# Macaron block on one core: score products in shared PSUM rows, and a reordered start

## The reference, cut to what matters

```python
x = x + 0.5 * ffn(layernorm(x))    # 8 experts, D = F = 256
x = x + attn(layernorm(x))         # 16 heads of 16, causal
x = x + 0.5 * ffn(layernorm(x))

# ffn, for every token and all 8 experts:
weights = golden_weights(sigmoid(x @ Wr / temperature))
h = silu(x @ Wg[e]) * (x @ Wu[e])
out = sum over e of weights[e] * (h @ Wd[e])

# attn:
scores = q @ k.T / sqrt(16), causal mask to -inf
attn   = softmax(scores) ; ctx = attn @ v ; out = ctx @ Wo.T + bo
```

## Time and profile before

| | |
|---|---|
| median of 3 runs | 751.4 us (751.22 to 753.1) |
| the profiled execution | 749.88 us, span 748.1 us |
| TensorE busy | 738.6 us, 99% of the span, 4712 products |
| VectorE busy | 477.6 us, 64% |
| GpSimd busy | 416.0 us, 56% |
| ScalarE busy | 348.8 us, 47% |
| DMA | 90.20 MB, mean 121 GB/s |

### The profile page before, as it was taken

How to read it: one execution, slowest core, us unless ns; L and a number is a source line. 1 busy time by engine, 2 the same in 40 slices (tenths; PEclk the granted TensorE clock), 3 DMA queues, 4 the chain that set the end, 5 groups by cost and what they waited for, 6 DMA issues and landing times.

```text
span 748.1 us, 13854 instructions
## 1 busy us (share of the span) xinstructions
PE 738.6 (99%) x4712; PEld 586.8 (78%) x4712; DVE 477.6 (64%) x1306; ACT 348.8 (47%) x663; POOL 416.0 (56%) x497
## 2 busy tenths in 40 slices
PE   7999999999999999999999999999999999999998
PEld 6888888777787777778777778777777788888887
DVE  6978855865667748578447756965658533584333
ACT  5446346243465543756435456444364552333322
POOL 2687484454663545844555753453564655556663
PEclk9999999999999999999999999999999999999999
DMA  9455224634233544234542423635332333223321
GB/s 276 157 183 177 90 94 127 180 111 142 71 105 121 160 128 117 73 106 133 159 143 72 136 69 107 187 98 168 92 91 86 96 105 110 85 71 128 109 103 56
DMA packets 69718, 90.20 MB, mean 121 GB/s; under 512 B 13200, under 2 KB 49424, under 8 KB 69648
## 3 DMA queue, kind: packets, MB, share of 16 engines
q1 hardware_dynamic: 67456, 89.01, 38.8%
q10 hardware_dynamic: 2192, 0.32, 0.3%
HBM read 72.10 MB, written 17.04 MB: 119 GB/s over the span
## 4 chain that ended last, share of the span: by engine, by line
PE 84%; DVE 4%; DMA 2%; SPq 2%; POOL 1%; issue 1%; ACT 0%; DVEq 0%; POOLq 0%; ACTq 0%
PE ra L795 14%; PE ra L797 13%; PE ra L796 13%; PE dn L817 8%; PE dn L818 7%; PE dn L819 7%; PE ra L923 5%; PE ra L896 5%; PE ra L911 4%; PE ra L760 2%; SPq L1469 1%; PE ra L874 1%; PE ra L887 1%; PE ra L876 1%; PE ra L875 1%; PE ra L888 1%
## 5 line engine op out<-in xcount | busy, mean ns | idle before, releaser
L1386 POOL TENSOR_TENSOR hid<-hid,wb 128x512 f32<-128x512 f32 x124 | 161.3, 1302 | 161.5 <-DVE hid L1242 152.8
L1390 POOL TENSOR_TENSOR ht_lo<-hid,ht_hi 128x512 fp32r<-128x512 f32 x124 | 162.3, 1311 | 110.9 <-ACT ht_hi L1025 110.7
L795 PE MATMUL ra<-xt_hi,wgu_hi 128*128 128x512 f32 x508 | 223.0, 439 | 0.4 <-DVE mx L1293 0.4
L797 PE MATMUL ra<-xt_lo,wgu_hi 128*128 128x512 f32 x508 | 200.7, 395 | 0.0
L796 PE MATMUL ra<-xt_hi,wgu_lo 128*128 128x512 f32 x508 | 200.6, 395 | 0.0
L1293 DVE CUSTOM_DVE_ANT_0 junk<-ra,mask 128x128 bf16<-128x128 f32 (+3 forms) x256 | 120.4, 486 | 73.9 <-PE ra L896 72.9
L817 PE MATMUL dn<-wd,ht_hi 128*128 128x256 f32 x512 | 161.6, 316 | 0.5 <-POOL ht_lo L1390 0.5
L1234 DVE SCALAR_TENSOR_TENSOR hid<-hid,ra 128x512 f32<-128x512 f32 x125 | 85.7, 686 | 115.7 <-ACT hid L1017 114.7
L818 PE MATMUL dn<-wd,ht_hi 128*128 128x256 f32 x512 | 143.7, 281 | 0.0
L819 PE MATMUL dn<-wd,ht_lo 128*128 128x256 f32 x512 | 143.5, 280 | 0.0
L1025 ACT ACTIVATE ht_hi<-hid 128x512 fp32r<-128x512 f32 x124 | 78.0, 629 | 123.9 <-POOL hid L1386 104.0
(11 more groups left out here) (161 smaller groups left out, 815.6 us busy)
## 6 DMA issues: line engine op xcount, KB each, us to landing
wd<-wd_parts SPq DMA_DIRECT2D x56, 512.0 KB, 3.8
wb<-wts_rows SPq DMA_DIRECT2D x62, 256.0 KB, 3.9
qk_parts<-parts SPq DMA_DIRECT2D x32, 192.0 KB, 2.3
q_st<-qk_parts SPq DMA_DIRECT2D x96, 64.0 KB, 2.5
k_st<-qk_parts SPq DMA_DIRECT2D x96, 64.0 KB, 2.3
wd_parts<-wd SPq DMA_DIRECT2D x8, 512.0 KB, 3.1
ctx_rows<-cx SPq DMA_DIRECT2D x16, 256.0 KB, 3.0
stage<-in_Wg SPq DMA_DIRECT2D x8, 256.0 KB, 4.4
```

The lines of the kernel that those rows point to most:

```text
L795: mm(b_, w_hi, xt_hi[q % 2][:, c, :], start=c == 0, stop=False)
L797: last = mm(b_, w_hi, xt_lo[q % 2][:, c, :], start=False, stop=c == KT - 1)
L1386: nc.gpsimd.tensor_tensor(tb, tb, wb[m % NWB][:, :], ALU.mult).then_inc(hw_done, 1)
L1390: nc.gpsimd.tensor_tensor(ht_lo[n % NHT][:, :], hidden(n)[:, :], f32(ht_hi[n % NHT][:, :]), ALU.subtract).then_inc(lo_done, 1)
```

## The change

- **Maxima in shared rows.** `MAX_ROWS` lays the 16 max products of a group in ten banks as the exponentials are: for two heads, five banks: 128 then 384 of one head (two such), 256 of one and 256 of the other, and 512 alone (two such). TensorE signals once a bank; VectorE reduces each part with an instruction of its own and frees the bank after the last.
- **Exp rows.** In `LAYOUT` the 128 columns now come ahead of the 384 in the bank's order of products; columns stay where they are.
- **First rows' second half.** `x_rest` is sent from ScalarE's queue, as its first DMA, and no longer from SP's.
- **Root step.** For the first batch, three root steps become one of the old kind and one of third order (one more unlinked and four linked instructions).
- **Three tiles on VectorE.** `("ln", 0, 0)` takes tiles 0, 1 and 2; ScalarE takes tile 3. The second pair's transposes wait for both.
- **First expert by halves.** High and low parts of gate and up are made for the first hidden half (`sg`), then for the second (`sgx`, behind the second pair's eviction on ScalarE and behind its low part on VectorE). Expert 1's high part follows the first down weights on ScalarE.
- **Planner.** PERIOD is 4.5 for 4.55, the assumed lengths of the changed items follow.

```diff
-LAYOUT = [[(0, 0, 0)], [(1, 0, 0)], [(0, 1, 0), (0, 3, 384)], [(1, 1, 0), (1, 3, 384)],
+LAYOUT = [[(0, 0, 0)], [(1, 0, 0)], [(0, 3, 384), (0, 1, 0)], [(1, 3, 384), (1, 1, 0)],
           [(0, 2, 0), (1, 2, 256)]]
+MAX_ROWS = [[(0, 0, 384), (0, 2, 0)], [(1, 0, 384), (1, 2, 0)], [(0, 1, 0), (1, 1, 256)], [(0, 3, 0)], [(1, 3, 0)]]
-M0, PERIOD = 27.6, 4.55
+M0, PERIOD = 27.6, 4.5
...
-            for k in range(GH * QT):
-                put(meet[g] - PERIOD + 0.15 + 0.27 * k if b + g else meet[0] - 2.1 + 0.115 * k, ("max", b, g, k))
+            for r in range(GB):
+                put(meet[g] - PERIOD + 0.15 + 0.43 * r if b + g else meet[0] - 2.1 + 0.184 * r, ("max", b, g, r))
...
+        if e == 0:
+            add("act", ("sg", 0), 0.55, ("sp", "ld", 0))
+            add("act", ("sgx",), 0.55, ("sp", "ld", 0), then=[("act", "xt", 0, 1)])
+            add("dve", ("sg", 0), 0.62, ("act", "sg", 0), port=True, then=[("dve", "ln", 0, 0)])
+            add("dve", ("sgx",), 0.62, ("act", "sgx"), port=True, then=[("dve", "xt", 0, 1)])
+        else:
+            add("act", ("sg", e), 1.0, ("sp", "ld", e), then=[("act", "sd", 0)] if e == 1 else [])
...
-            row = (0.232, 0.232, 0.285, 0.285, 0.236)
+            row = (0.232, 0.232, 0.235, 0.235, 0.236)
...
                     if kind == "max":
-                        mm(o[:, 0:(i + 1) * P], q_st[0:KROWS, G % NST, hh, i * P:(i + 1) * P],
-                           k_st[0:KROWS, G % NST, hh, 0:(i + 1) * P], start=True, stop=True).then_inc(ra_full, 1)
+                        for hp, i, c in MAX_ROWS[r % PB]:
+                            hh = 2 * pr + hp
+                            last = mm(o[:, c:c + (i + 1) * P], q_st[0:KROWS, G % NST, hh, i * P:(i + 1) * P],
+                                      k_st[0:KROWS, G % NST, hh, 0:(i + 1) * P], start=True, stop=True)
+                        last.then_inc(ra_full, 1)
...
             def _(act):
+                act.dma_start(x_res[:, 2:QT, :], A["x"][0].rearrange("(i p) d -> p i d", p=P)[:, 2:QT, :]).then_inc(x_rest, 16)
                 act.dma_start(stage_r[:, :, 0:E], A["Wr"].rearrange("(k p) e -> p k e", p=P)).then_inc(wr_in, 16)
...
-                        for _ in range((2, 1)[it[2]]):
+                        if it[2] == 0:
                             link(nc.vector.tensor_tensor(tmp, y, v, ALU.mult))
                             link(nc.vector.scalar_tensor_tensor(out=tmp, in0=tmp, scalar=-0.5, in1=y, op0=ALU.mult,
                                                                 op1=ALU.mult))
                             link(nc.vector.scalar_tensor_tensor(out=y, in0=tmp, scalar=1.5, in1=y, op0=ALU.add,
                                                                 op1=ALU.mult))
+                        else:
+                            nc.vector.tensor_scalar(shift[:, tile], y, 0.375, None, ALU.mult)
+                            link(nc.vector.tensor_tensor(tmp, y, v, ALU.mult))
+                            link(nc.vector.tensor_tensor(tmp, tmp, y, ALU.mult))
+                            link(nc.vector.scalar_tensor_tensor(out=tmp, in0=tmp, scalar=-10.0 / 3.0, in1=tmp, op0=ALU.add,
+                                                                op1=ALU.mult))
+                            link(nc.vector.scalar_tensor_tensor(out=y, in0=tmp, scalar=5.0, in1=shift[:, tile], op0=ALU.add,
+                                                                op1=ALU.mult))
...
                     if it == ("ln", 0, 0):
-                        for i in range(2):
-                            nc.vector.tensor_scalar(xn[0][:, i, :], x_res[:, i, :], mv[:, i, 0:1], rstd[:, i:i + 1],
+                        for i in range(3):
+                            nc.vector.tensor_scalar(xn[i // 2][:, i % 2, :], x_res[:, i, :], mv[:, i, 0:1], rstd[:, i:i + 1],
                                                     ALU.subtract, ALU.mult).then_inc(first_xn, 1)
...
+                    if kind == "sgx":
+                        dve.wait_ge(g_hi, 2)
+                        nc.vector.tensor_tensor(halves_of(wgu_lo[:, 0, :, :], 1), halves_of(stage[0][:, :, 0:2 * F], 1),
+                                                halves_of(f32(wgu_hi[:, 0, :, :]), 1), ALU.subtract).then_inc(g_lo, 1)
...
+                        for hp, i, c in MAX_ROWS[r % PB]:
+                            w, col = (i + 1) * P, (2 * (r // PB) + hp) * QT + i
+                            ins = nc.vector.tensor_tensor_reduce(
+                                out=junk[:, k % NJUNK, c:c + w], in0=o[:, c:c + w], in1=mask[:, T - w:T], scale=1.0,
+                                scalar=-3.0e38, op0=ALU.add, op1=ALU.max, accum_out=mx[(b * GR + g) % 2][:, col:col + 1])
+                        ins.then_inc(freed, 1)
...
                             sp.dma_start(x_res[:, 0:2, :], rows[:, 0:2, :]).then_inc(x_in[0], 16)
-                            sp.dma_start(x_res[:, 2:QT, :], rows[:, 2:QT, :]).then_inc(x_rest, 16)
```

More of the change, by code:

```diff
@@ L109, in schedule @@
         sg = (-9.46, -8.8, 0.4, 3.3, 5.2, 7.6, 9.3, 11.0)[e]
-        sd = (0.55, 0.9)[e] if e < NWD else down[FT * (e - NWD) + FT - 1] + 0.42
+        sd = (-8.85, 0.9)[e] if e < NWD else down[FT * (e - NWD) + FT - 1] + 0.42
         put(sg, ("sg", e))
+        if e == 0:
+            put(-8.9, ("sgx",))
         put(sd, ("sd", e))
@@ L385, in plan @@
         head = [("dve", "xt", q, 0), ("dve", "xt", q, 1)] if n % CB == 0 else []
-        low = [("pool" if m in BY_POOL["sg"] else "dve", "sg", m)] if q == 0 and n % FT == 0 else []
+        low = [("pool" if m in BY_POOL["sg"] else "dve", "sg", m)] if q == 0 and n % FT == 0 else [("dve", "sgx")] if n == 1 else []
         if n == 0:
@@ L504, in plan @@
             add("sp", ("st", b, g), 5.0, ("sp", "ql", b, 1, 1 if g < 2 else 3), slot, kb=768)
-            width = (0.11, 0.118, 0.175, 0.232)
             time = (0.31, 0.44, 0.57, 0.70)
[L507 to L510, removed]
+            for r in range(GB):
+                add("pe", ("max", b, g, r), 0.24, ("sp", "st", b, g), ("pe", "mt") + ago(2) if G >= 2 else None)
+                add("dve", ("max", b, g, r), sum(time[i] for _, i, _ in MAX_ROWS[r % PB]), ("pe", "max", b, g, r))
+            add("pe", ("mt", b, g), 0.12, ("dve", "max", b, g, GB - 1))
             add("act", ("mt", b, g), 0.22, ("pe", "mt", b, g), ("act", "mx") + ago(1) if G else None)
@@ L740, in hidden, with halves_of @@
             return first_hid[n] if n < NHID else hid[n % NHID]
+        def halves_of(ap, f):
+            return ap.rearrange("p k (s f c) -> p k s f c", s=2, f=FT)[:, :, :, f, :]
         def gate_low(e):
             mine = BY_POOL["sg"]
-            return (pool_g_lo, mine.index(e) + 1) if e in mine else (g_lo, e + 1 - sum(k < e for k in mine))
+            return (pool_g_lo, mine.index(e) + 1) if e in mine else (g_lo, e + 2 - sum(k < e for k in mine))
         def down_low(e):
@@ L779, in _ @@
                             pe.wait_ge(*emptied(("xt", q, 1)))
-                        if q == 0 and f == 0 and not first and not s:
+                        if n == 0 and not first and not s:
+                            pe.wait_ge(g_lo, 1)
+                        if n == 1 and c == 0 and not s:
+                            pe.wait_ge(*gate_low(0))
+                        if q == 0 and f == 0 and n > 0 and c == 0 and not s:
                             pe.wait_ge(*gate_low(e))
@@ L981, in _ @@
                             act.wait_ge(ra_full, full(XN_BEFORE[it]))
-                        for i in range(2):
+                        for i in range(1 if it == ("ln", 0, 1) else 0, 2):
                             ins = normalise(xn[m][:, i, :], b * QT + 2 * m + i)
@@ L1292, in _ @@
                         dve.wait_ge(ra_full, full(it))
-                        nc.vector.tensor_tensor_reduce(out=junk[:, k % NJUNK, 0:w], in0=o[:, 0:w], in1=mask[:, T - w:T], scale=1.0,
-                                                       scalar=-3.0e38, op0=ALU.add, op1=ALU.max,
-                                                       accum_out=mx[(b * GR + g) % 2][:, s:s + 1]).then_inc(freed, 1)
+                        for hp, i, c in MAX_ROWS[r % PB]:
[4 more added lines that the diff above has]
+                        ins.then_inc(freed, 1)
                     if kind == "mt":
```

55 lines of the change are left out of this document (35 added, 20 removed).

## The result

The changed kernel takes 744.32 us, the median of four runs (742.7 to 745.51), beside 752.25 for the kernel before (four runs); the ratio is 0.9893, 95% interval 0.9866 to 0.9920. Run once more later, beside 17 runs of the kernel before, it gave 744.04 against 751.51, 0.9908 (0.9889 to 0.9926). The forecast was 746.5 and 0.9935; the measured time lies near the low end of its range of 743.8 to 750.2, and the gain of 7 to 8 us is some one and a half times the 4.9 of the sum. The profiled execution took 745.51, the slowest of its four, where that of before (749.88) was a short one; so the two traces differ by 4.4 us, the medians by 7 to 8.

What follows compares the result with a forecast made beforehand. TensorE's stream was taken as the bound, 732.4 of 748.1 us. Stream -5.5, head +0.6, tail and small waits 0 sum to -4.9; from the median of 751.4 that gives 746.5 us, ratio 0.9935, range 743.8 to 750.2.

Steps and rivals of the forecast that it cites:

- Score rows: TensorE's stream: max products in shared rows, the 128 first in every row, save 5.5 us together.
- The order's part: Score rows: with the 128 first, 47 exp rows go from 0.285 to 0.235 us each, 2.4 us.
- third term: Max rows: the second of 32 pairs of 256, with the other 20 products of 128, saves some 0.5 us.
- Rival 3: VectorE's two-reduction rows hold a bank TensorE needs, or delay transposed maxima: at most 23 us in all; chance 0.08.
- the sign of being wrong: Profile after: waits of TensorE for VectorE's maxima beyond 1 us would show the forecast wrong.
- The head: Time before the first real product, 12.08 us: the change adds 0.6 us, all from the warm-up's start.
- rival 1: Head: the first half of x shares DMA evenly with the second, +1.25 us, 747.2 in all; chance 0.10.
- The +1.25: Head: under even sharing, x's first half lands with the second, 256 KB at 210 GB/s, 1.25 us later.
- the +0.6: Head: later warm-up start from x's second half on ScalarE's queue, the middle between 0 and 1.25 us.
- an earlier chain gains 0: Head: the shorter chain from x to the transposes saves 0 us, because TensorE's warm-up covers it.
- rival 2: Head: the clock rises sooner after warm-up's start, half of 1.3 us comes back, 745.2 in all; chance 0.10.
- PERIOD "nothing": Planner: PERIOD 4.5 for 4.55 only draws the same work 16 x 0.05 chunks earlier, costed at nothing.

## Why the prediction was right, and where not

**Score rows: right, mis-sized.** The order's part came out as worked out: 2.6 us measured for 2.4 in the exp rows. The whole term, -5.5, is too small. By medians rows with PERIOD 4.55 save 9.2 us (751.51 to 742.28). Between traces, the changed kernel's busy time, the half-clock stretch put back, fell by 7.6. Summed over every place where score rows stand between f32 products (start to second f32 product, less 0.12 or 0.235), the cost fell from 79.6 us in the kernel before to 72.6 and 72.7 in the two kernels with 4.55, so 7.0, of which 0.8 are waits that fall in them; the whole stream fell by 8.0 there.

In the medians over all such rows a max row of 128 and 384 costs 0.228 against 0.296 apart, so 44 of them 3.0 for the 2.6 of the working; an exp row 0.227 against 0.284, so 47 of them 2.7 for 2.4. That makes 5.7 of the 7.0; what the third term put at 0.5, pairs of 256 and the other 128s, comes to about 1.3 with those waits. Where the last us of the stream comes from I can't show; the rest of the 9.2 can be that the profiled execution of before was 1.5 us under its median.

**VectorE's longer rows: right alone, not with the new PERIOD.** Rival 3 had two forms. No entry names a bank held by a reduction, so the 0.24 us a row is covered. But the transposed maxima came late once, by the 2.0 (1.8 in the second profile): the sign of being wrong, a wait for maxima beyond 1 us, did show. The longer rows alone don't make it: with the same rows and 4.55 no profile has it, nor has the old kernel with 4.5. It needs both, by way of the place of `den` in SP's queue.

**The head: two steps failed, the term is small.** The first is the price of the second queue. The halves of x, issued together, landed within 0.4 to 0.5 us of each other in all seven profiles with two queues, about as rival 1's even sharing had it. First the DMA view of the changed kernel (KB, us from issue to landing), then windows of the kernel before and of the changed one (the last three columns are clock, DMA share and GB/s):

```profile
x_res<-in_x ACTq DMA_DIRECT2D x1, 256.0 KB, 3.6
x_res<-in_x SPq DMA_DIRECT2D x1, 256.0 KB, 3.2
```

```profile
2.60:4.20 1.60, 0.39 (x2) 0.42 (x3) 0.50 (x2) 0.00 (x0) 1.43 (x4) 1.00 0.86 226
2.60:4.20 1.60, 0.11 (x1) 0.14 (x1) 0.22 (x1) 0.00 (x0) 1.43 (x4) 1.00 1.04 360
```

The +1.25 took 210 GB/s from the earlier trace rows for what the engines can move; over these 1.6 us, other transfers included, they moved 315 to 360 in the seven profiles with two queues and 226 to 283 in the seven with one. So the first half came only 0.28 us later here, 0.4 on the mean (4.16 for 3.77, seven profiles with each queue), for the +0.6 taken, a middle between two bounds that came near by luck and not by a mechanism; and the second half came sooner, at 4.6 for 5.3 on the mean. The Trainium skill (DMA: Bandwidth & Descriptors, "Issuing engines are not separate DMA queues") has such transfers interleave; the trace agrees, with the two landings 0.4 us apart.

The second is "an earlier chain gains 0". It holds when the 32 warm-up products take some 6 us or more (12.18 against 12.08), and not when the fast ones begin sooner and they take 5.3 to 5.8: then the new chain starts the first product at 11.38 to 11.50 (three profiles), the old one at 11.84 to 12.50 (three). That is rival 2's mechanism, in part of the executions, and nothing in the change causes it: short and long warm-ups occur with either start. In the changed kernel the first real product stood 7.3 us behind the first warm-up product, not the 8.3 that I had named. On the mean the first product starts at 11.84 in the six profiles with the new start and all 32 warm-up products (without the one with SP's queue alone), at 12.12 in six with the old. So the head's term is near -0.3, for +0.6; alone it can't be told from nothing.

**PERIOD "nothing": wrong.** With the new rows it costs 2.2 us (0.9908 to 0.9879 with the old head; with the new 2.3 or 1.1, by the changed kernel's second or first ratio). The step looked only at how early the same work is drawn. The 0.05 of a chunk also changed the order on SP's queue and on VectorE, and with it what stands behind what. Moving one load back did not recover the time. What of the tighter order costs the 1 to 2 us stays open; at least two links (`den` to `mp` to `q_st`, and `ct_lo`) each hold TensorE in turn.

**The sum.** -9.2 for the rows, +2.2 for PERIOD, -0.3 for the head make -7.3; measured -6.9 and -8.0. The forecast was nearer than its terms were, since a stream 3.7 us too small met a price of PERIOD that was left out. The forecast of -4.9 came within 0.6 us of the traces' difference (-4.4) since the two profiled executions lie on opposite sides of their medians, an agreement that proves little.

## What to carry over

Where short bf16 products are sprinkled between f32 ones, cost each by the start of the second f32 product behind it, and put the shortest product of a row anywhere but last. When a planner's constant changes, compare the order that it writes on every queue, DMA queues too, before costing it at nothing; and when a wait is removed, ask which wait of the same length comes next. A start that hangs on a clock rise has two critical paths: read it from several executions.

## What was unexpected of the hardware

- A bf16 product of 256 columns ahead of an f32 product took as long as one of 128: 0.24 us to the second f32 product for both.
- 2.0 us of idle TensorE at 268 us was followed by 3.5 us at a granted clock of 0.51, about as dear as the wait; in the changed kernel's second profile a wait of 1.8 us at the same place left a granted clock of 0.88 over 265 to 275 us; with the second half on SP's queue the wait there was 1.3 us, with `den` first one of 1.4 stood some 15 us later, and the clock stayed at 1.00 in both.
- Two transfers of 256 KB issued together from SP's and ScalarE's queues landed 0.4 to 0.5 us apart, and from 2.6 to 4.2 us the DMA engines moved 315 to 360 GB/s; behind each other on SP's queue, with 0.5 us between their issues, the statistics of the second began 1.3 to 2.0 us behind those of the first, at 226 to 283 GB/s.
- The same warm-up of 32 products took 5.3 to 6.7 us over the profiles; with the new start the first product began anywhere between 11.38 and 12.30 by it.
